# Side work of a layer-0 attention moved to other units, and a queue of loads reordered, in a two-layer transformer kernel on one core

## The reference

```python
x = _layernorm(x + _L0_attn_ref(x, ...))   # 16 heads of 128, causal softmax
x = _layernorm(x + _L0_ffn_ref(x, ...))    # 8 experts of 176, top 2, and a shared branch of 704
x = _layernorm(x + _L1_attn_ref(x, ...))   # 16 heads of 16, 4 key/value groups, no mask
x = _layernorm(x + _L1_ffn_ref(x, ...))    # 16 experts of 176, top 6, and a shared branch of 352
```

```python
probs = softmax(x @ gate_w.T);  top_w, top_i = top_k(probs, 2);  top_w /= top_w.sum(-1)
moe = sum over the 2 chosen experts e of top_w[e] * ((silu(x @ w_gate[e]) * (x @ w_up[e])) @ w_down[e])
shared = (silu(x @ sw_gate) * (x @ sw_up)) @ sw_down
out = moe + shared * sigmoid(x @ shared_gate_w)
```

## Time and profile before

| | |
|---|---|
| runs of the kernel (3) | 2110.42, 2114.85, 2118.72 us; median 2114.85 us |
| the profiled execution | 2106.45 us, its span 2104.7 us |
| mean granted TensorE clock | 0.986 of full |
| busy | PE 2010.0 us (95%), PEld 1546.6 (73%), DVE 1416.4 (67%), ACT 1209.7 (57%), POOL 627.4 (30%) |

### The profile page before, as it was taken

How to read it: one execution, slowest core, us unless ns; L and a number is a source line. 1 busy time by engine, 2 the same in 40 slices (tenths; PEclk the granted TensorE clock), 3 DMA queues, 4 the chain that set the end, 5 groups by cost and what they waited for, 6 DMA issues and landing times. The chain is left out here.

```text
span 2104.7 us, 34444 instructions
## 1 busy us (share of the span) xinstructions
PE 2010.0 (95%) x12163; PEld 1546.6 (73%) x12163; DVE 1416.4 (67%) x2853; ACT 1209.7 (57%) x2488; POOL 627.4 (30%) x739
## 2 busy tenths in 40 slices
PE   8999999999999999998899789999999999999997
PEld 6888888888888888886788454333334788778886
DVE  5666667766666776665657368999993557645555
ACT  5666666665565566665445246888886434444343
POOL 3444444443343355454342230000000112222221
PEclk9999999999999999999999889999999999999999
DMA  2310000000000000004253211000000111111111
GB/s 76 110 47 13 21 21 21 21 21 9 21 21 13 21 31 26 21 24 105 88 161 106 63 42 33 18 23 20 21 9 1 52 38 46 38 46 46 47 52 58
DMA packets 74221, 86.90 MB, mean 41 GB/s; under 512 B 12443, under 2 KB 54086, under 8 KB 74054
## 3 DMA queue, kind: packets, MB, share of 16 engines
q1 hardware_dynamic: 70982, 76.32, 12.7%
q0 software_dynamic: 3072, 8.39, 1.3%
HBM read 58.32 MB, written 18.35 MB: 36 GB/s over the span
## 5 line engine op out<-in xcount | busy, mean ns | idle before, releaser
L1141 POOL TENSOR_TENSOR a_pr<-a_pr,a_rinv 128x512 f32<-128x512 f32 (+3 forms) x384 | 312.7, 829 | 463.8 <-DVE a_rinv L1398 463.7
L91 PE MATMUL psum<-xh,g_hi_gu 128*128 128x512 f32 x744 | 306.2, 412 | 11.3 <-PEq L59 3.8
L2845 ACT ACTIVATE a_pt<-psum 128x512 f32<-128x512 f32 x512 | 276.3, 597 | 59.2 <-PE psum L2745 36.6
L2864 DVE TENSOR_REDUCE x_m_negm<-psum 128x1 f32<-128x1024 f32 x240 | 290.7, 1223 | 13.7 <-PE psum L2730 11.3
L93 PE MATMUL psum<-xh,g_lo_gu 128*128 128x512 f32 x744 | 293.0, 394 | 0.0
L92 PE MATMUL psum<-xl,g_hi_gu 128*128 128x512 f32 x744 | 292.3, 393 | 0.0
L1489 POOL TENSOR_TENSOR g_lo_gu<-g_raw_gu,g_hi_gu 128x512 fp32r<-128x512 f32 x62 | 80.2, 1294 | 632.3 <-ACT g_hi_gu L1485 631.3
L1303 ACT ACTIVATE a_pr<-psum,a_negm 128x128 f32<-128x128 f32 (+7 forms) x256 | 190.3, 743 | 116.2 <-DVE a_negm L1388 112.7
L1310 ACT ACTIVATE a_pth<-psum 128x512 fp32r<-128x512 f32 (+3 forms) x384 | 174.9, 490 | 112.9 <-PE psum L1207 108.8
L1405 DVE TENSOR_TENSOR a_ptl<-psum,a_pth 128x512 fp32r<-128x512 f32 (+3 forms) x384 | 201.1, 551 | 2.4 <-ACT a_pth L1310 2.0
L1388 DVE CUSTOM_DVE_ANT_0 psum<-psum,a_mask 128x128 f32<-128x128 f32 (+7 forms) x256 | 191.8, 750 | 5.0 <-PE psum L93 3.8
(11 more groups left out here) (403 smaller groups left out, 4695.8 us busy)
## 6 DMA issues: line engine op xcount, KB each, us to landing
g_raw_gu<-in_gu SPq DMA_DIRECT2D x60, 256.0 KB, 2.7
g_raw_gu<-in_qkv SPq DMA_DIRECT2D x32, 256.0 KB, 2.8
f_raw_dn<-in_down SPq DMA_DIRECT2D x60, 128.0 KB, 2.0
xs<-a_mask SPq DMA_DIRECT2D x2, 2944.0 KB, 10.8
ys<-e_yb SPq DMA_DIRECT2D x46, 128.0 KB
a_wvr<-in_qkv SPq DMA_DIRECT2D x32, 128.0 KB, 2.4
a_wor<-in_o SPq DMA_DIRECT2D x32, 128.0 KB, 2.0
x_queries_qq<-x_qhi SPq DMA_DIRECT2D x128, 32.0 KB, 2.0
```

Source lines behind the costliest of these rows:

```text
L91: pe.matmul(out, a_hi, b_hi, start=first, stop=False)
L1141: pool.tensor_tensor(x, x, rinv[:, j:j + 1].to_broadcast([P, count * P]), ALU.mult).then_inc(p_done, 1)
L2845: act.activation(pt[:, s % SLOTS, g, :], st_ps[:, n % 3, :], ACT.Exp, scale=1.0 / HD1).then_inc(exp_done, 1)
L2864: dve.tensor_reduce(negm[:, u % 2, g * NQ + q:g * NQ + q + 1], mx_ps[:, bank, :, :], AX.XY, ALU.max, negate=True).then_inc(mx_taken, 1)
```

## The change

In a0 the side tasks are grouped into 20 places, at the head of the task list of units 0 and 4 of turns 17 to 26 (before the pv product of the unit), and the scatters stand in units 3 and 6 of turns 26 to 29. The dealing tasks "pick" and "weigh" are cut into "share", "best", "reject", "choose"; "cw" stands after "map"; in e0 they hang on steps 1 to 9. In f0 the last logits stand one place sooner and "ex" two half-steps sooner. In f2 `load` is cut in two; the gate/up loads of tiles 2 and 3 go ahead, the queries follow, the down tile 2, then the keys; the gathers begin at K = 0 and the additions stand in the loop; the maxima begin a chunk later, at (2, 1), and end at K = 6; the "gs" tasks stand at K = 2 to 5. (Line numbers in it are those of the diff.)

```diff
--- before.py
+++ after.py
@@ -584,11 +584,22 @@
                 dve.wait_ge(ring.emptied, ring.count(key))
                 chain(dve.tensor_reduce(self.mx[:], self.lg[:, :, 0:ne], AX.X, ALU.max))
                 dve.tensor_tensor(self.sh[:], self.lg[:, :, 0:ne], spread(self.mx[:]), ALU.subtract).then_inc(self.shifted, 1)
-        elif kind == "weigh":
+        elif kind == "share":
+            dve.wait_ge(self.exp_done, self.exp0 + 1)
+            chain(dve.tensor_reduce(self.sm[:], self.ex[:], AX.X, ALU.add))
+            chain(dve.reciprocal(self.sm[:], self.sm[:]))
+            chain(dve.tensor_tensor(self.pr[:], self.ex[:], spread(self.sm[:]), ALU.mult))
+            chain(dve.tensor_copy(self.bi[:], self.pr[:]))
+        elif kind == "best":
+            for k in range(n):
+                i = dve.max(self.top[:, k, :], self.bi[:, k, :])
+            chain(i)
             chain(dve.memset(self.top[:, :, TOP0:8], 3.0e38))
+        elif kind == "reject":
             for k in range(n):
                 i = dve.match_replace(self.rest[:, k, :], self.top[:, k, :], self.bi[:, k, :], -3.0e38)
             chain(i)
+        elif kind == "choose":
             chain(dve.tensor_tensor(chosen[:], chosen[:], self.bi[:], ALU.not_equal))
             dve.tensor_copy(self.mask[:, 0:n, :], chosen[:]).then_inc(self.masked, 1)
         elif kind == "cw":
@@ -880,7 +891,7 @@
 BACK = [("nb", s) for s in range(4)]
 CHOOSE = [("lg", 0), ("lg", 1), ("lt",), ("ex",), ("pick",), ("weigh",)]
 LOGITS = [("lg", n) for n in range(S // P)]
-DEAL = [("ex",), ("pick",), ("weigh",), ("cw",), ("rk",), ("row",), ("map",), ("part",)]
+DEAL = [("ex",), ("share",), ("best",), ("reject",), ("choose",), ("rk",), ("row",), ("map",), ("cw",), ("part",)]
 
 
 def enlist(ring, tasks):
@@ -905,13 +916,16 @@
     MASKED = -1.0e30
 
 
-    SIDE = ([(norm, t) for t in FORE + [("std",), ("xn", 0), ("xn", 1)] + BACK] + [(router, t) for t in LOGITS + DEAL])
-    SPOTS = [(hb, qt) for hb in range(H0 + 1, H0 + 8) if hb % 4 for qt in (1, 2, 3, 4, 6)]
-    assert len(SPOTS) >= len(SIDE)
+    SIDE = ([[(norm, t)] for t in FORE] + [[(norm, ("std",)), (norm, ("xn", 0))], [(norm, BACK[0]), (norm, ("xn", 1))]] +
+            [[(norm, t)] for t in BACK[1:]] + [[(router, t) for t in LOGITS[n:n + 2]] for n in range(0, len(LOGITS), 2)] +
+            [[(router, (t,)) for t in ts] for ts in (("ex", "share"), ("best", "reject"), ("choose",), ("rk",), ("row",), ("map", "cw"),
+                                                     ("part",))])
     HOSTED = {}
-    SCATTER0 = H0 + 8
-    for (hb, qt), (side, t) in zip(SPOTS, SIDE):
-        HOSTED.setdefault(hb, []).append((qt, side, t))
+    SCATTER = {}
+    for n, tasks in enumerate(SIDE):
+        HOSTED[H0 + 1 + n // 2, n % 2 * CQ] = tasks
+    for n in range(NQ):
+        SCATTER[H0 + 10 + n // 2, (3, 6)[n % 2]] = n
 
     VALUES = [(0, qt, 0, qt) for qt in range(VT)] + [(0, 7, 1, 0), (1, 3, 1, 1), (1, 5, 1, 2), (1, 7, 1, 3)]
     for g in range(2, HB // VG):
@@ -932,8 +946,8 @@
         for at, qt, g, i in VALUES:
             if at == hb:
                 units[qt].append(("v", i, g))
-        for qt, side, t in HOSTED.get(hb, ()):
-            units[qt].append(("side", side, t))
+        for qt in (0, CQ):
+            units[qt] = [("side", side, t) for side, t in HOSTED.get((hb, qt), ())] + units[qt]
         if last:
             units.append([("pv", 1, False), ("o", 1, False, 0), ("o", 1, False, 1)])
         return units
@@ -1170,10 +1184,10 @@
                     if (hb, qt) == (1, 5):
                         constants.gpsimd(pool)
                         router.clear(pool)
-                    if hb >= SCATTER0 and qt == 6 and hb - SCATTER0 < router.TILES:
-                        if hb == SCATTER0:
+                    if (hb, qt) in SCATTER:
+                        if SCATTER[hb, qt] == 0:
                             pool.wait_ge(zeroed, 16 * B)
-                        router.scatter(pool, xs[0], hb - SCATTER0)
+                        router.scatter(pool, xs[0], SCATTER[hb, qt])
 
         @block.tensor
         def _(pe):
@@ -2089,11 +2103,12 @@
 
         @block.sync
         def _(sp):
-            def load(K):
+            def load_gu(K):
+                sp.wait_ge(gu.lo_done, K0 + K - 1)
+                gu.load(sp, K0 + K, TILE[K])
+
+            def load_dn(K):
                 if K >= 2:
-
-                    sp.wait_ge(gu.lo_done, K0 + K - 1)
-                    gu.load(sp, K0 + K, TILE[K])
                     sp.wait_ge(lo_dn_done, K0 + K - 1)
                 if PAIRED[K]:
                     for x in (LOW, HIGH):
@@ -2103,20 +2118,21 @@
 
             if experts:
                 experts.load(sp, 0)
-            load(0)
-            load(1)
+            load_dn(0)
+            load_dn(1)
             if experts:
                 experts.load(sp, 1)
                 experts.load_down(sp)
-            if not experts:
-                load(2)
-                load(3)
+            else:
+                load_gu(2)
+                load_gu(3)
             for o in begins:
                 if isinstance(o, FirstMaxima):
                     o.queries.first(sp, o.side, ring)
             for K in range(2, NT):
                 if K >= 4 or experts:
-                    load(K)
+                    load_gu(K)
+                load_dn(K)
                 if experts:
                     experts.load(sp, 2 * K - 2)
                     experts.load(sp, 2 * K - 1)
@@ -2149,13 +2165,12 @@
                         experts.remainder(pool, j)
                 if gathered is not None:
                     for c in range(NC):
-                        n = (K - 1) * NC + c
-                        if 0 <= n < NormHalf.TILES:
+                        n = K * NC + c
+                        if n < NormHalf.TILES:
                             pool.wait_ge(gate_done, N0 + K * NC + c + 1)
                             gathered[0].gather(pool, gathered[1], n)
-            if gathered is not None:
-                for s in range(NormHalf.GROUPS):
-                    gathered[0].add(pool, s)
+                    if K >= 2:
+                        gathered[0].add(pool, K - 2)
 
         @block.tensor
         def _(pe):
@@ -2377,7 +2392,7 @@
             enlist(ring, plan[at])
         block = ph.block()
 
-        SCATTER = [5 + 3 * n // 2 for n in range(DealHalf.TILES)]
+        SCATTER = [6 + 4 * n // 3 for n in range(DealHalf.TILES)]
         GATHER = [NT + 3 + 3 * n // 2 for n in range(NormHalf.TILES)]
 
         def stores(slot, n):
@@ -3040,7 +3055,7 @@
                     experts = Experts(e, "ex", w0, slots[3].rearrange("p (s t) d -> p s (t d)", s=2))
                     r0a.after = r0b
                     plan = {(2, 0, 1): tasks(n0b, [("std",), ("xn", 0)]), (2, 1, 1): tasks(n0b, [("xn", 1)]),
-                            (6, 1, 1): tasks(r0b, LOGITS[7:] + DEAL[:1])}
+                            (6, 0, 0): tasks(r0b, LOGITS[7:]), (6, 1, 0): tasks(r0b, DEAL[:1])}
                     for n in range(NormHalf.GROUPS):
                         plan[n // 2, n % 2, 1] = tasks(n0b, FORE[n:n + 1])
                         plan[3 + n // 2, n % 2, 0] = tasks(n0b, BACK[n:n + 1])
@@ -3076,9 +3091,9 @@
                             (0, 1, 0): tasks(x0, [("pj", 2, 1)]), (0, 1, 1): tasks(x0, [("vt", 0)]),
                             (1, 0, 0): tasks(x0, [("pj", 0, 1)]), (1, 0, 1): tasks(x0, [("vt", 1)])}
                     for n in range(m0.COUNT):
-                        plan[2 + n // 4, n // 2 % 2, n % 2] = [(m0, (0, n)), (m0, (1, n))]
-                    for n, at in enumerate(((4, 1, 1), (5, 0, 1), (5, 1, 1), (6, 1, 1))):
-                        plan[at] = plan.get(at, []) + [(n1b, ("gs", n))]
+                        plan[2 + (n + 2) // 4, (n + 2) // 2 % 2, n % 2] = [(m0, (0, n)), (m0, (1, n))]
+                    for n in range(NormHalf.GROUPS):
+                        plan[2 + n, 0, 1] = plan.get((2 + n, 0, 1), []) + [(n1b, ("gs", n))]
                     shared_half(nc, "f2", counters, 1, w0, gu0, xh, xl, yT, idr, eps, psum, signals, r0b, None, plan, (x0, m0),
                                 gathered=(n1b, ys[1]))
```

## The result

The kernel before took 2112.64 us (median of 4 runs, 2107.66 to 2118.72), the changed one 2083.22 us (4 runs, 2079.84 to 2084.64): ratio 0.9857, 95% interval 0.9834 to 0.988, 29.4 us less. The forecast was 2082 us. The span of the profiled execution went from 2104.7 to 2082.7 us, 22.0 us less; the forecast made that 32.9. The stages say where the 11 us are.

A forecast was written before the change was run, and what follows sets the result against it. PE, busy 95% of the span, was taken as the bound, with dispersed stalls in a0 and a queue-made hole in f2. Gains 10.6 + 0.6 + 1.5 + 17.8 + 2.4 = 32.9 us gave 2082 us; range 2070 to 2096.

The forecast's parts named there:

- a0: Side tasks in a0: cost falls from 26.8 to 16.2 us, 10.6 us gained; bounds 0 and 17.2.
- some 4: Sign in a0: a turn with two logit pairs takes some 4 us over a plain turn.
- cover beneath the value product: In a0, DVE idles 3.84 us in unit 0 during the long pv; side tasks at its head are covered.
- Rival 1: In a0, leads stall PE as much as the ends did; a0 gains nothing, 2093 us; chance 0.10.
- The scatters: Moved scatters in a0, hidden by POOL: cost 0, at worst 2 us.
- f0: End of f0: earlier logits let exponentials run between the two takings of y; 0.6 us gained, bounds 0 and 1.7.
- e0: Dealing steps in e0: half of 3.2 us absorbed, 1.5 us gained; nine steps at about 2.3 us each.
- f2, the hole: In f2, keys issued about 1163: PE's 13.7 us wait and 4.1 us of half clock go, 17.8 us gained.
- f2, the end: End of f2: ACT's copies close it instead of POOL's additions; 2.4 us gained, bounds 0 and 2.9.
- f2, the additions: POOL's additions inside f2's loop: cost 0, at worst 4 us; beside DVE some 3 us, not from PE.
- Rivals 2 to 4: (2) keys late anyway, 2094 or 2100 us, 0.09; (3) slower, 2125 us, 0.02; (4) no change, 2106 to 2114, 0.03.

The follow-up runs named there:

- e7: Changed kernel with a0's side work at the end of units 0 and 4 instead of ahead of their value products; 2091.07 us, ratio 0.9909.
- e10: Changed kernel with a0's side work still leading unit 0 but at the end of unit 4; 2075.36 us, ratio 0.9867.
- e11: Changed kernel with a0's side work still leading unit 4 but at the end of unit 0; 2077.57 us, ratio 0.9896.
- e1: Kernel before with only a0's part of the change; f0, e0 and f2 as before; 2089.63 us, ratio 0.9942.
- e2: Kernel before with only SP's changed load list in f2 (query and key pieces queued before SP waits for POOL); 2080.94 us, ratio 0.9942.
- e3: Changed kernel with POOL's addition ahead of the four gathers of its tile instead of behind them; 2072.89 us, ratio 0.9853.
- e12: Changed kernel with e0's scatters starting two tiles later, at the eighth, one a tile; 2067.98 us, ratio 0.9845.
- e4: Changed kernel with e0 as before: dealing of half 1 in seven steps instead of nine, scatters from the fifth tile; 2073.98 us, ratio 0.989.
- e6: Changed kernel with POOL's addition ahead of the gathers and the first maxima at their old places; 2074.81 us, ratio 0.9835.
- e5: The changed kernel itself, unaltered, timed again on another chip; 2081.87 us, ratio 0.987.
- e8: Changed kernel with POOL's addition ahead of the gathers, timed beside the unaltered changed kernel on one chip; 2079.26 us, ratio 0.9843.

## Why the prediction was right, and where its steps were not

**a0** (forecast 26.8 to 16.2, 10.6 gained): ten turns cost 299.89 - 10 x 28.37 = 16.2 us over plain ones, from 26.8; right. That the number is met to a tenth is luck, since the split was off both ways by 2.4 us: idle 4.2 and not 6.6, busy 12.0 over and not 9.6. The split of the cost before was off too. The forecast called 17.2 of the 26.8 us stalls, but in those seven turns PE was idle for 11.8 us (225.41 - 213.63 in the earlier trace rows); the other 15 are busy time, of which a stretch of 3.4 us at 1.2 GHz (from 554.8 on) makes about 1.7. So of the 10.6 us 7.4 are idle time (11.9 to 4.6 in ten turns) and 3.3 busy. Turn 22 was 3.7 over where "some 4" stood. I put the gain down to cover beneath the value product; e7, e10 and e11 bear that out, more strongly than I weighed it. Rival 1 is refuted. The scatters (0) cost nothing that can be seen: from turn 27 to f0 a0 took 147.99 us, for 148.74 before.

**f0** (0.6): the end went from 9.43 (last silu at 1015.23 to e0 at 1024.66) to 9.25 us (1005.37 to 1014.62), 0.2 gained. What was lost lies earlier: ACT waited for the third gate/up tile:

```profile
964.46 0.63 ACT L1499 ACTIVATE g_hi_gu<-g_raw_gu 128x512 fp32r<-128x512 f32 x1 [6.44 <-DMA g_raw_gu<-in_gu]
```

Before that wait was 5.56 us. PE's wait behind it was 1.2 before, 2.1 after, 1.4 in e1 and 1.5 in e2, which have f0's side tasks as before, and 1.7 to 4.0 in e3 to e12: a landing that varies, for which the forecast had no term. Whether the change moved it is not known.

**e0** (1.5): the dealing steps were right as far as they go. From the second to the ninth of DVE's `e_hid` they took 16.00 us (1021.21 to 1037.21), 2.29 a step, where 2.3 stood. But what follows gives part of it back: in e3 against e4 the same steps took 1.9 us less (16.04 for 17.94), the next eight 0.9 more (17.91 for 17.03). So the term was mis-sized, 0.5 to 1 us for 1.5, where no hole hides it. In the first profile the stage did not get shorter at all, because the hole at the scatters' start grew, from waits of 0.47 and 1.71 us to

```profile
1043.87 0.41 PE L2463 MATMUL psum<-ident,e_xt 128*128 128x128 f32 x2 [3.37 <-issue]
1045.31 0.66 PE L2481 MATMUL psum<-ident,e_hid 128*128 128x128 f32 x2 [1.03 <-DVE e_shl L2569]
```

and the clock was 1.2 GHz for 6.8 us behind it (3.4 before). On the other chips no such hole was there, in either form of e0. Its cause stays open.

**f2, the hole** (17.8): the keys left at 1152.53, which is 1161.7 on the old time base (f2 began 9.2 us sooner), for 1163.1 forecast; the 13.7 us went. The clock's 4.1 came in e2 (6.7) and not in the changed kernel's own profile. The steps that were off are not in this term but in the next two.

**f2, the end** (2.4): closing by ACT's copies is worth 4.3 us (p1's wait 5.71 to 1.42) and the `f_hh` wait 0.9 more, and the last maxima cost 1.4 (in e6, with the old places, that wait is gone and 0.8 for `f_hh` is back). Together 3.8 us.

**f2, the additions** (0): this is the step that failed, a cost that the forecast had put at nothing. I had them beside DVE at "some 3 us from DVE, not from PE", by one row of 1.37 us, which shows one POOL instruction and not two. (The 4 us "at worst" were for another way, a late remainder that PE's next tile waits for; no such wait came.) They cost PE 2.19 and 2.13 us in the first profile and 2.2 us once in the six others, because POOL's remainder follows the addition without a gap and DVE's subtraction waited out both. The sum of f2's idle time: -13.7 - 4.3 - 0.9 + 5.4 (maxima waits 2.3 to 7.7) = -13.5, for 13.6 measured (23.4 to 9.8). The clock did the rest: it was 1.2 GHz from 1177.6 for 3.4 us, from 1194.6 for 3.4 and from 1208.3 for 20.5, each time within 2 us of the end of a wait of PE of 2 us. Not every such wait has it: the one of 1.96 us that ended at 1205.24 in e5 did not. With one of the long subtractions less, as in e5, f2 took 78.42 us for the 77.9 that the forecast makes of 98.12 (98.12 - 17.8 - 2.4).

The Trainium skill, SBUF — State Buffer, section "Summary: rules for kernel authors", has the second to issue, of a VectorE instruction with two SBUF inputs and a GpSimd one that reads SBUF, block until the first finishes. The trace agrees for one POOL instruction beside it (1.33 to 1.37 us for 0.69), and goes further for two in a row: the subtraction waited for the second as well, though that began 0.85 us after it.

**The sum.** The median fell by 29.4 us where the forecast had 32.9; that 2082 nearly met 2083.22 owes something to the reference, as four runs gave 2112.64 for the before and three had given 2114.85. Rivals 2 to 4 did not occur: the keys were in time, also beside the gathers.

## What to carry to other kernels

Put side work where the engine that it loads is idle, and ahead of the long product that covers it: here the same pieces in the same units cost 12.4 us more at the end. When work moves to an engine that shares something with the critical one, look at what stands directly before and behind it: a subtraction beside one POOL instruction cost PE nothing, one beside an addition glued to a remainder cost it 2.2 us, and four gathers between those two took the wait away. Take a stretch apart into idle and busy time of the bound engine before explaining it; the lower clock behind a wait can be as large as the wait, and comes and goes between runs of one program.

## What the runs showed of the hardware that was not expected

DVE's 128x512 subtraction of two SBUF tiles: 0.68 to 0.69 us alone and beside POOL's indirect gathers (e8, 1173.55), 1.33 to 1.37 beside one elementwise POOL instruction, 2.60 to 2.71 beside two without a gap.

One program's f2 took 78.42 and 85.33 us, with PE busy for 70.26 and 75.50 us on the same instructions; the difference in busy time is the granted clock. A change that saves PE 2 us of waiting can so be lost in one execution: e8's f2 had 2.3 us less idle time than e5's and took 2.7 us longer. e0 took 112.4 to 114.5 us in eight profiles on two chips and 122.7 to 123.8 in six others, with about 5 and 12 us of idle time of PE; what separates them is not known.
